# A 32-slot gated delta-rule loop: gates step by step, split norm statistics, narrowed inverse products, a second output bank, reordered slots and idle products

## What is computed

```python
x = x + GatedDeltaAttention(layernorm(x))   # 16 heads, DK=64, DV=128
x = x + layernorm(x) @ sign(W).T
x = x + CausalAttention(layernorm(x))       # 16 query heads, 4 kv heads
x = x + MoE(layernorm(x))                   # 8 experts, top 2, DFF=512
```

```python
S = a_t * (S - b_t * outer(k_t, k_t @ S)) + outer(k_t, v_t)
o_t = S.T @ q_t
```

## Time and profile before

| | us |
|---|---|
| median of three runs | 1827.51 |
| lowest and highest | 1818.52, 1835.88 |
| run that was profiled | 1827.64 |
| its span, first to last instruction | 1825.9 |
| PE busy in it | 1657.6 |
| DVE busy | 1242.2 |
| ACT busy | 803.4 |

### The profile page before, as it was taken

One profiled execution on the slowest core, in us unless ns is written; L12 is line 12 of the kernel. 1 busy time (PEld: TensorE's weight loads), 2 busy tenths in 40 slices (PEclk: granted clock), 3 DMA queues, 4 the chain that ended last, 5 costly groups with the idle time before them and its releaser, 6 DMA issues.

```text
span 1825.9 us, 32512 instructions
## 1 busy us (share of the span) xinstructions
PE 1657.6 (91%) x12563; PEld 999.0 (55%) x12563; DVE 1242.2 (68%) x2261; ACT 803.4 (44%) x1403; POOL 484.2 (27%) x986
## 2 busy tenths in 40 slices
PE   5778899999999999999999998898899899989998
PEld 1124666666665665666666666633455454544555
DVE  5947788888877878787767667555655764765443
ACT  5736456565556564555444444322233223323221
POOL 1023544535345354354435353000000000000000
PEclk9868899999999999899999999979999999999999
DMA  3000000000000000000000014000000000000000
GB/s 107 1 8 17 9 9 17 9 17 9 12 14 9 16 9 9 14 11 9 17 14 12 15 34 147 1 0 1 1 1 1 6 1 1 5 3 1 1 6 6
DMA packets 61338, 26.42 MB, mean 14 GB/s; under 512 B 54001, under 2 KB 57905, under 8 KB 60801
## 3 DMA queue, kind: packets, MB, share of 16 engines
q1 hardware_dynamic: 61184, 24.34, 5.2%
HBM read 16.40 MB, written 7.34 MB: 13 GB/s over the span
## 4 chain that ended last, share of the span: by engine, by line
PE 73%; DVE 13%; ACT 7%; issue 6%; SPq 1%; DMA 1%; POOL 0%; DVEq 0%; ACTq 0%
PE bank L795 6%; PE bank L779 6%; PE bank L501 6%; PE bank L782 6%; PE bank L535 4%; PE bank L592 4%; PE bank L481 3%; PE bank L524 3%; PE bank L451 3%; PE bank L483 3%; PE bank L619 2%; PE bank L742 2%; PE bank L431 2%; PE bank L421 2%; PE bank L545 2%
## 5 line engine op out<-in xcount | busy, mean ns | idle before, releaser
L1648 POOL TENSOR_TENSOR SU<-SU 128x28 f32<-128x28 f32 (+6 forms) x448 | 204.6, 457 | 35.1
L1271 DVE TENSOR_TENSOR AM<-bank,et 128x512 f32<-128x512 f32 x192 | 126.7, 688 | 126.8 <-PE bank L501 94.4
L1644 POOL TENSOR_TENSOR SU<-SU 128x28 f32<-128x28 f32 (+6 forms) x448 | 198.9, 444 | 35.2
L978 ACT ACTIVATE et<-bank 128x512 f32<-128x512 f32 x192 | 114.8, 598 | 207.7 <-PE bank L483 182.8
L1623 POOL TENSOR_TENSOR st<-st,nh 128x4 f32<-128x4 f32 x16 | 16.6, 1035 | 559.3 <-DVE st L1175 535.7
L1198 DVE SCALAR_TENSOR_TENSOR vc<-vy,conv,vc 128x512 f32<-128x512 f32 x192 | 148.8, 775 | 6.4 <-ACT vc L926 1.9
L795 PEld LDWEIGHTS bank<-WQ,AM 128*128 128x128 f32 x1024 | 129.2, 192 | 32.4 <-issue 24.9
L795 PE MATMUL bank<-WQ,AM 128*128 128x128 f32 x1024 | 138.0, 279 | 3.6 <-DVE X L1521 3.6
L779 PE MATMUL bank<-xnT,KQ 128*128 128x512 f32 x256 | 136.7, 616 | 0.0
L782 PE MATMUL bank<-xnT,KQ 128*128 128x512 f32 x256 | 132.5, 600 | 2.1 <-DVE AM L1511 2.1
L1640 POOL MEMSET SU<- 128x32 f32 x32 | 5.0, 155 | 482.1 <-DMA SU<-scratch 482.1
(11 more groups left out here) (217 smaller groups left out, 3449.2 us busy)
## 6 DMA issues: line engine op xcount, KB each, us to landing
scratch<-AM SPq DMA_DIRECT2D x128, 48.0 KB, 1.8
SM<-SM SPq DMA_DIRECT2D x288, 2.0 KB
SU<-scratch SPq DMA_DIRECT2D x128, 32.0 KB
WQ<-in_wqkv_dram SPq DMA_DIRECT2D x1, 2048.0 KB, 8.8
KQ<-in_wg_dram SPq DMA_DIRECT2D x4, 512.0 KB, 8.3
KQ<-in_wu_dram SPq DMA_DIRECT2D x4, 512.0 KB, 9.0
WQ<-in_wd_dram SPq DMA_DIRECT2D x1, 2048.0 KB, 15.5
WQ<-in_wo_dram SPq DMA_DIRECT2D x1, 1024.0 KB, 9.4
```

Source lines behind the costliest of these rows:

```text
L978: e.activation(et[:, q % 2, :], bank[2][:, :], ACT.Exp).then_inc(s_exp, 1)
L1271: e.tensor_tensor(dst, bank[(3, 1)[hh]][:, :].rearrange("p (k t) -> p k t", k=2), et[:, q % 2, :].rearrange("p (k t) -> p k t", k=2), ALU. ...
L1644: e.tensor_tensor(tmp[:, :, 0:k, 0:15 - k], sub[:, :, 0:k, k:k + 1].to_broadcast([128, 2, k, 15 - k]), sub[:, :, k:k + 1, k + 1:16].to_bro ...
L1648: e.tensor_tensor(sub[:, :, 0:k, k + 1:16], sub[:, :, 0:k, k + 1:16], tmp[:, :, 0:k, 0:15 - k], ALU.subtract).then_inc(s_su, 1)
```

## The change

- `gates2` on DVE is cut into its five steps; one runs in each of the slots with s % 8 from 3 to 7, ahead of `vfin(2g)`.
- A norm's `bn_stats` run ahead of `vfin(2g)` in the slot before the norm, the rest where all of it ran.
- `inv_a` makes only the even column blocks of its product, `inv_b` only the odd ones, L538 32 of 64 columns; `inv_y` subtracts only these.
- `ksel` writes its k sums with two products of 16 columns (partitions 0 and 32) in place of one of 64; the constant `sel` gets narrower.
- `out(j,1)` and its `ot` use bank 1 for groups below 29. `out(j,1)` no longer waits for `ot(j,0)` there, and `gram(g,0)` waits for `ot` of group g-3.
- PE's order in a slot: `gram(g,0)` ahead of `decay(g,0,1)`, `inv_a(j,1)` ahead of `decay(g,1,0)`, `gram(g,1)` ahead of `decay(g,1,1)`, `vproj(2g)` ahead of `inv_d(j)`.
- Idle products where slots 9 to 11 have no group j or w yet: 22 in slots 9 and 10 each, 4 in slot 11. The four ahead of `out(j,1)` in late slots go. Four more products in the prologue set banks 7 and 4 to zero.

```diff
--- before.py
+++ after.py
@@ -44,7 +44,7 @@
...
         lmask = sb("lmask", [128, 2, 64])
-        sel = sb("sel", [128, 78])
+        sel = sb("sel", [128, 30])
         wab = sb("wab", [128, 96])
@@ -189,6 +189,10 @@
...
+        def obank(n, hh):
+            return bank[1 if hh and n < NN - 3 else 6]
         def wbank(n, hh):
@@ -423,12 +427,13 @@
...
                 i8, kq, p = (t // 2) % 8, t % 2, t // 16
-                rows, o = (bank[7][64:80, :], 16) if kq else (bank[7][0:64, :], 64)
                 if p and i8 == 0:
...
-                e.matmul(rows, sel[:, 14 - 2 * i8:14 - 2 * i8 + o], squares_of(t), start=i8 == 0, stop=i8 == 7).then_inc(s_ksel, 1)
+                for o in ((64,) if kq else (0, 32)):
+                    ins = e.matmul(bank[7][o:o + 16, :], sel[:, 14 - 2 * i8:30 - 2 * i8], squares_of(t), start=i8 == 0, stop=i8 == 7)
+                ins.then_inc(s_ksel, 1)
@@ -492,6 +497,8 @@
...
                         e.wait_ge(s_x, 8 * (n - 3))
+                    if n >= 3:
+                        e.wait_ge(s_ot, 2 * (n - 3) + 2)
                 if n or i:
@@ -509,6 +516,11 @@
...
                     e.matmul(bank[7][96:128, :], identb[:, 0:32], idle[:, :], start=True, stop=True)
+            def half(a, lv, odd):
+                m = 16 << lv
+                return a.rearrange("p (x y t) -> p x y t", y=2, t=m)[:, :, odd, :]
@@ -521,8 +533,8 @@
...
                         pq = slice(64 * q, 64 * q + 64)
-                        ins = e.matmul(bank[4][pq, j * 64:j * 64 + 64], block_of(n, j, q, 64 * q), XP[pq, j, :],
-                                       start=True, stop=True)
+                        ins = e.matmul(half(bank[4][pq, j * 64:j * 64 + 64], lv, 0), block_of(n, j, q, 64 * q),
+                                       half(XP[pq, j, :], lv, 0), start=True, stop=True)
                 ins.then_inc(s_ia, 1)
@@ -532,10 +544,11 @@
...
                         pq = slice(64 * q, 64 * q + 64)
-                        ins = e.matmul(bank[5][pq, j * 64:j * 64 + 64], PP[pq, j, :], YP[pq, j, :], start=True, stop=True)
+                        ins = e.matmul(half(bank[5][pq, j * 64:j * 64 + 64], lv, 1), PP[pq, j, :], half(YP[pq, j, :], lv, 1),
+                                       start=True, stop=True)
                 if lv == 1:
                     for j in range(NJ):
-                        ins = e.matmul(bank[4][0:64, j * 64:j * 64 + 64], YP[0:64, j, :], PP[0:64, j, :],
+                        ins = e.matmul(bank[4][0:64, j * 64:j * 64 + 32], YP[0:64, j, :], PP[0:64, j, 0:32],
                                        start=True, stop=True)
@@ -585,9 +598,13 @@
...
                     e.wait_ge(s_u2, n + 1)
+                elif n >= NN - 3:
+                    e.wait_ge(s_ot, 2 * n + 1)
                 else:
-                    e.wait_ge(s_ot, 2 * n + 1)
-                b = bank[6]
+                    e.wait_ge(s_am, 6 * (n + 2) + 6)
+                    if n:
+                        e.wait_ge(s_x, 8 * n)
+                b = obank(n, hh)
                 for bt in range(2):
@@ -646,7 +663,12 @@
...
                 if t == 2:
                     e.wait_ge(s_set, NS_SET - 1)
+                    for o in (0, 32, 64):
+                        e.matmul(bank[7][o:o + 32, :], identb[:, 0:32], idle[:, :], start=True, stop=True)
+                    e.matmul(bank[4][:, :], identb[:, :], idle[:, :], start=True, stop=True)
                 if t >= 2:
@@ -827,50 +849,59 @@
...
                 if 0 < g <= NN: vtr(2 * g - 1)
+                if has_g: gram(g, 0)
                 if has_g: decay(g, 0, 1)
-                if has_g: gram(g, 0)
                 more(s, 0)
+                if has_j: inv_a(j, 1)
+                elif j < 0: fill(2)
+                more(s, 1)
                 if has_g: decay(g, 1, 0)
-                if has_j: inv_a(j, 1)
-                more(s, 1)
                 if has_w: squares(w)
                 more(s, 2)
+                if has_g: gram(g, 1)
                 if has_g: decay(g, 1, 1)
-                if has_g: gram(g, 1)
                 if has_j: inv_b(j, 1)
+                elif j < 0: fill(4)
                 more(s, 3)
...
                 if has_j: inv_c(j)
+                elif j < 0: fill(2)
                 more(s, 4)
...
                 if gap(s, "signed") is not None: signed_mm(gap(s, "signed"), bank[0], s_vV, 2 * g)
+                if has_g: vproj(2 * g)
                 if has_j: inv_d(j)
-                if has_g: vproj(2 * g)
+                elif j < 0: fill(2)
                 if has_g: vproj(2 * g + 1)
...
                 if has_w: wout(w, 0)
+                elif w < 0: fill(2)
                 if has_j: solve1(j)
+                elif j < 0: fill(2)
                 more(s, 5)
...
                 if has_w: wout(w, 1)
+                elif w < 0: fill(2)
                 if has_p: kproj(2 * s + 2)
                 if has_j: solve2(j)
+                elif j < 0: fill(2)
                 more(s, 6)
...
                 if has_j: solve3(j)
+                elif j < 0: fill(2)
                 more(s, 7)
...
                 if has_j: out(j, 0)
+                elif j < 0: fill(2)
                 more(s, 8)
                 if has_g: vtr(2 * g)
-                if has_g and not has_p: fill(4)
                 if has_j: out(j, 1)
@@ -1008,8 +1039,8 @@
...
                     e.wait_ge(s_ms, n)
-                e.activation(qb[:, hh, :], bank[6][:, :], ACT.Square).then_inc(s_osq, 1)
-                e.activation(OT(n)[:, hh, :], bank[6][:, :], ACT.Copy).then_inc(s_ot, 1)
+                e.activation(qb[:, hh, :], obank(n, hh)[:, :], ACT.Square).then_inc(s_osq, 1)
+                e.activation(OT(n)[:, hh, :], obank(n, hh)[:, :], ACT.Copy).then_inc(s_ot, 1)
@@ -1155,18 +1186,23 @@
...
         def _(e):
-            def norm(key):
+            def norm(key, part=0):
                 i = NI[key]
                 _, _, t0, w, _ = NORMS[i]
-                if key[0] == "sg":
+                if part == 2:
+                    pass
+                elif key[0] == "sg":
                     e.wait_ge(s_x, 8 * NG * (key[1] + 1))
...
                 st6, mv, rs = (s[:, o:o + k * 4].rearrange("p (k w) -> p k w", k=4) for o, k in ((0, 6), (24, 2), (32, 2)))
-                for k in range(w):
-                    ins = e.bn_stats(st6[:, k, :], X[:, t0 + k, :])
-                ins.then_inc(s_nst, 1)
+                if part < 2:
+                    for k in range(w):
+                        ins = e.bn_stats(st6[:, k, :], X[:, t0 + k, :])
+                    ins.then_inc(s_nst, 1)
+                if part == 1:
+                    return
                 e.wait_ge(s_nst, i + 1)
@@ -1227,17 +1263,23 @@
...
-            def gates2(p):
+            def gates2(p, k):
                 d = 7 * p
-                e.wait_ge(s_ga, 6 * p + 6)
-                e.scalar_tensor_tensor(gl, gx, 0.0, gl, ALU.max, ALU.add).then_inc(s_gd, 1)
-                e.wait_ge(s_gd, d + 3)
-                e.tensor_scalar(gl, gl, gate[:, 4:5], None, ALU.mult).then_inc(s_gd, 1)
-                e.scalar_tensor_tensor(gE, gB, 0.0, gE, ALU.min, ALU.subtract).then_inc(s_gd, 1)
-                e.wait_ge(s_gd, d + 4)
-                e.tensor_tensor_scan(gc, reset, gl, 0.0, ALU.mult, ALU.add).then_inc(s_gd, 1)
-                e.wait_ge(s_gd, d + 6)
-                e.scalar_tensor_tensor(gc[32:48, :], gE, 0.6931471805599453, gc[32:48, :], ALU.add, ALU.add).then_inc(s_gd, 1)
+                if k == 0:
+                    e.wait_ge(s_ga, 6 * p + 6)
+                    e.scalar_tensor_tensor(gl, gx, 0.0, gl, ALU.max, ALU.add).then_inc(s_gd, 1)
+                elif k == 1:
+                    e.wait_ge(s_gd, d + 3)
+                    e.tensor_scalar(gl, gl, gate[:, 4:5], None, ALU.mult).then_inc(s_gd, 1)
+                elif k == 2:
+                    e.scalar_tensor_tensor(gE, gB, 0.0, gE, ALU.min, ALU.subtract).then_inc(s_gd, 1)
+                elif k == 3:
+                    e.wait_ge(s_gd, d + 4)
+                    e.tensor_tensor_scan(gc, reset, gl, 0.0, ALU.mult, ALU.add).then_inc(s_gd, 1)
+                else:
+                    e.wait_ge(s_gd, d + 6)
+                    e.scalar_tensor_tensor(gc[32:48, :], gE, 0.6931471805599453, gc[32:48, :], ALU.add, ALU.add).then_inc(s_gd, 1)
@@ -1292,12 +1334,15 @@
...
                 e.wait_ge(s_ib, 2 * n + lv + 1)
-                e.tensor_tensor(YP[:, :, :], YP[:, :, :], wide(bank[5]), ALU.subtract).then_inc(s_iy, 1)
+                odd = lambda a: a.rearrange("p (j y t) -> p j y t", y=2, t=16 << lv)[:, :, 1, :]
+                y = odd(flat(YP[:, :, :]))
+                e.tensor_tensor(y, y, odd(bank[5][:, :]), ALU.subtract).then_inc(s_iy, 1)
                 if lv == 0:
...
                 else:
-                    e.tensor_tensor(XP[0:64], XP[0:64], wide(bank[4])[0:64], ALU.subtract).then_inc(s_id, 1)
```

(13 more changed lines are left out.)

## The result

| | before | after |
|---|---|---|
| median of 20 runs, us | 1829.38 | 1823.94 |
| lowest and highest | 1818.52, 1838.50 | 1802.19, 1853.96 |
| run that was profiled | 1827.64 | 1802.19 |
| its span, mean granted clock | 1825.9, 0.952 | 1800.4, 0.945 |

The ratio is 0.993, 95% interval 0.990 to 0.996: 13 us by that ratio, 5.4 by the medians. The ratio is taken over the faster executions alone and leaves out after's six slowest and none of before's; over all twenty of each it is 0.997. The forecast was 1777, range 1752 to 1818. By the ratio the sign is right; the size is not: less than 1% faster, where the prediction gave 0.80 to a time under 1809.

A forecast was written before the change was run, and what follows sets the result against it. TensorE (PE), busy 91% of the span, was taken as the bound. Terms -33.4 - 25.6 - 19.2 - 3 + 14 + 3 + 14 + 0 = -50.2 took 1827.5 to 1777 us, range 1752 to 1818.

The forecast's parts named there:

- The sums: ksel's three 16-wide products run together in slots 12 to 31, 2.04 becoming 1.08: -19.2 us.
- the narrowed `inv_a`: Part of the narrowed products: the stationary load sets the pace, so five groups a slot save only -3 us together.
- the gates steps: One DVE step ahead of vfin(2g) in five slots brings slots 12, 20 and 28 down to 30.87: -25.6 us.
- the idle products of the first slots: Idle products in slots 9 to 11: gains and costs sum to 0, bounds +10 and -15 us.
- my rival at 1716: Narrowed products pay by the columns streamed, a further 61 us off 1777; chance 0.05.
- The wait at the slot's head: PE waits of 0.74 and 0.70 a slot go, a new one of 0.28 before gram(g,0) comes: sum -33.4 us.
- late next: The step asking what becomes late: gram(g,0) waits 0.28 for bank 1's copy ot(j,1); nothing more stalls.
- the wait moves: Rival: gram(g,0) or DVE behind it loses in every slot what was won, 1810; chance 0.11.
- the forecast 17: inv_d behind vproj(2g): +14 us over eleven slots with special steps, +3 for clock falls in norm slots.
- two falls, +14: Narrowed products decay(g,1,1) to decay(g,2,0): two clock falls over the loop at 7 us each.
- a rival with 0.10: The narrowed stretch lets the clock fall in slot after slot; every second slot would give 1868; chance 0.10.
- the bound that I had set for "wrong": The prediction would be wrong with a clock below 1.00 in more than eight of slots 13 to 40.

The follow-up runs named there:

- e3_invd_wide: The changed kernel with inv_d ahead of vproj(2g) again and inverse products and subtractions at full width: 1765.64 us, ratio 0.967 to before.
- e4_gates: The kernel before with only the gates' five DVE steps spread over five slots and the norm statistics split: 1803.25 us, ratio 0.989.
- e2_wide: The changed kernel with inv_a, inv_b, the L538 product and the subtractions at full width again: 1791.39 us, ratio 0.981 to before.
- e1_invd: The changed kernel with inv_d(j) ahead of vproj(2g) again, narrowed products kept: 1810.62 us, ratio 0.990 to before.
- e5_narrow: The kernel before with only the narrowed inverse products and halved subtractions: 1853.90 us, ratio 1.011.
- e10_cover: As e3_invd_wide, with inv_a(j,1) moved ahead of vtr(2g-1): 1762.95 us, ratio 0.963 to before.
- e8_nofill: As e3_invd_wide, without the 48 idle products of slots 9 to 11: 1766.73 us, ratio 0.964 to before.
- e14_wide_b: As e1_invd, with inv_b, its second product and the subtractions at full width, inv_a still narrowed: 1760.54 us, ratio 0.963 to before.
- e16_wide_a: As e1_invd, with inv_a at full width, inv_b, its second product and the subtractions still narrowed: 1796.29 us, ratio 0.978 to before.

## Why the prediction was wrong

**What bounds, and the small terms: right.** The sums run together (2.04 to 1.05, forecast 1.08), the narrowed `inv_a` saves next to nothing (1.05 to the next start for the 1.08 of `e3_invd_wide`), the gates steps give slots 12, 20 and 28 back (each 30.87 in `e4_gates`), the idle products of the first slots do nothing. My "sixteen products" of rows 6 are sixteen instructions, two to a product; the comparison stands, since both sides were counted so. `inv_a` at full width, in slot 17 of `e3_invd_wide`:

```profile
339.80 1.15 PE L536 MATMUL bank<-XP,AM 64*64 64x64 f32 x32
```

The Trainium skill (TensorE: Matmul & The Clock Gate, LDWEIGHTS) prices the load by the stationary columns alone. That halving the moving ones left 1.05 of 1.08 agrees with it. Its formula by the moving columns (same page, Back-to-back issue gap), on which the 64 us and my rival at 1716 went, is given there for an isolated product, and the table under it has one price for 1 to 64 columns; the estimate took neither into account. No run here shows such a saving.

**The wait at the slot's head: mis-sized.** Forecast 0.28 for `gram(g,0)`, measured 0.72 to 0.76 for `vtr(2g-1)`. The step that failed is "late next". I looked at what the moved product itself waits for, bank 1, and not at what ACT had done while PE waited for `out(j,1)`. `vtanh` and `vfin` stand behind the copy `ot(j,0)` that PE waited for, and had been in time only because PE stood still too. The plain slot takes 28.96 for the 28.7 forecast, the part -28 for -33.4; the rival *the wait moves* came half true, 0.72 of 1.44.

**`inv_d`: near in size alone, partly by luck.** +15 for the forecast 17. It costs nothing in slots 18 and 26 and more than 1.07 in the five norm slots of the loop, each of which has a longer fall or a new one: 19.9 where I had 5 x 1.07 + 3 = 8.4. In the trace the norm and signed slots add up to 24, and 7.6 less in slot 28 and 2.4 less in slots 9 to 12, which this part wasn't meant to change, bring that down to 14.7 at the start of slot 40. On the changed order at full width it costs 25 (`e2_wide` against `e3_invd_wide`). That the shortened slots have less slack is my reading, not shown.

**The clock in the narrowed stretch: the main miss.** I charged two falls, +14, and called the case of many falls a rival with 0.10. Alone on the kernel before, narrowing costs 20 instead of 11; on the changed order with `inv_d` in its place it costs 40 (`e1_invd` against `e3_invd_wide`). The price of one fall was too high, 7 for 4.6 (33.59 for 28.96 in slot 17). The count was too low, and it isn't one number: the executions of after range over 50 us. I argued from slot 17, which holds 1.00 at full width, that PE without idle time is safe, although showed 20.4 us at 0.50 without idle time. That row, though a wait of 2.37 stands before it, should have had the weight. I also looked for falls only from slot 13 on: narrowing makes slot 11 6 us longer (42.05 in `e5_narrow`, 36.25 before, 31 to 36 in the full-width kernels but `e10_cover`, 41.46), which cancelled the gain of slot 12.

**The sum.** The three good parts alone multiply to 0.963, which `e8_nofill` (0.964) and `e3_invd_wide` (0.967) meet: these add. With narrowing and `inv_d` as measured alone the product is 0.982, 1797. After is 0.993. So of the 47 us between 1777 and 1823.94, some 18 are parts mis-sized when taken alone (+5 gates, +5 bank and order, +9 narrowing, -2 `inv_d`, the rest rounding), some 20 come from the parts costing more together than alone, narrowing above all. The remaining 9 are the difference between ratio and medians, and 1.9 of another median for before. That in after's narrowed kernel `inv_d` behind `vproj(2g)` costs only 6 (by intervals that overlap, so perhaps nothing) has a likely reason: it takes 1.07 of thin products out of the stretch and lets the wide `vproj` come sooner. That is argued, not shown. Open too is which of the other parts, the shorter sums or the order, doubles the price of narrowing.

**The profiled run.** Its -25.5 against the forecast -50.2 divides otherwise, since it has few falls in the narrowed stretch: slots 9 to 12 give 0.6 instead of 12, the slots with a norm, gates or signed step cost 33 for 17 against what a plain slot gained (15 by 5.0, 21 by 4.1, 26 by 4.1, 29 by 5.7, 37 by 6.1, six others by 1 to 2), the plain slots miss 0.25 each. Eight of the slots 13 to 40 are below 1.00 in it, which is just the bound that I had set for "wrong".

## What to carry to other kernels

An edit that takes streamed columns out of PE without taking time out saves nothing and, as here, can cost the clock; look for the stretch of the loop with the thinnest products, keep its width, and take idle products there as a test. When a wait on the bounding engine is removed, follow the lists of the other engines through the time of that wait: what they did in it is the next wait, of nearly the same size. And when a kernel's executions scatter with the granted clock, a profile of one of them, above all the fastest, is not the kernel.

## What the runs showed of the hardware

- The clock fell, and stayed at 0.50, while PE was busy without a gap: 10.20 us in slot 34 of after, 9.3 us behind the last wait, and 17.10 in `e5_narrow`, there 1.2 us behind a wait of 2.24. Slot 17 held 1.00 at full width in the same time (29.04 for 28.96) and with two idle products in it (29.55), and fell to 0.85 in `e1_invd`.
- A group of 32 instructions with 64 stationary columns takes 1.12 at 32 moving columns (354.21 of after) and 1.15 at 64 (339.80 of `e3_invd_wide`).
- Which of two like products is narrowed matters: the ratio is 0.967 with neither (`e3_invd_wide`), 0.963 with `inv_a` alone (`e14_wide_b`), 0.978 with `inv_b` alone (`e16_wide_a`) and 0.990 with both (`e1_invd`).
- Three sums of 16 columns at columns 0, 32 and 64 take 1.05 together where a 64-wide and a 16-wide one took 2.04, though the third sums other squares.
